# A Perceiver block on one core: the last 65 keys of the first attention as two products of 128 and 97 rows in place of three of 65

## The reference

```python
q = (query @ Wq + bq).reshape(B, L, NKV, G, HDIM)        # 8, 64, 8, 4, 128
k_, v_ = jnp.split(kv @ Wkv + bkv, 2, axis=-1)
scores = jnp.einsum('blkgd,bmkd->bkglm', q, k) * scale
attn = jax.nn.softmax(scores, axis=-1)
o = jnp.einsum('bkglm,bmkd->blkgd', attn, v).reshape(B, L, NHEAD * HDIM)
return o @ Wo + bo
```

## Time and profile before

| | us |
|---|---|
| median of 3 runs (2602.84 to 2605.58) | 2604.69 |
| profiled execution, device time | 2604.12 |
| its span, first to last instruction | 2602.3 |

### The profile page before, as it was taken

How to read it: one execution, slowest core, us unless ns; L and a number is a source line. 1 busy time by engine, 2 the same in 40 slices (tenths; PEclk the granted TensorE clock), 3 DMA queues, 4 the chain that set the end, 5 groups by cost and what they waited for, 6 DMA issues and landing times. The chain is left out here.

```text
span 2602.3 us, 42744 instructions
## 1 busy us (share of the span) xinstructions
PE 2497.1 (96%) x17160; PEld 2293.5 (88%) x17160; DVE 1726.8 (66%) x1956; ACT 1489.4 (57%) x2597; POOL 1348.7 (52%) x1009
## 2 busy tenths in 40 slices
PE   8999999999999999999999999999999599899878
PEld 6899999999999999999999999999987477654557
DVE  4157766777667776677766777667656699743473
ACT  3356655666556665566655666556543677523572
POOL 3335575485565558548556555854600599300352
PEclk9999999999999999999999999999999699999899
DMA  6520011111111101111111110100351300287200
GB/s 221 191 76 31 28 57 52 43 52 54 32 51 51 45 28 58 52 44 51 52 34 51 53 42 26 60 26 29 104 182 54 130 1 1 67 302 266 71 2 17
DMA packets 106989, 181.30 MB, mean 70 GB/s; under 512 B 8852, under 2 KB 72660, under 8 KB 105004
## 3 DMA queue, kind: packets, MB, share of 16 engines
q1 hardware_dynamic: 98476, 170.23, 19.7%
q10 hardware_dynamic: 8320, 8.39, 0.9%
HBM read 158.57 MB, written 20.02 MB: 69 GB/s over the span
## 5 line engine op out<-in xcount | busy, mean ns | idle before, releaser
L474 POOL TENSOR_TENSOR xa_pt_lo<-xs_st,xa_pt_hi 128x1024 fp32r<-128x1024 f32 x255 | 508.4, 2029 | 489.7 <-ACT xa_pt_hi L691 489.7
L54 PE MATMUL ctx_kv_ps<-ctx_wv_hi,ctx_hi 128*128 128x256 f32 x1536 | 431.8, 281 | 0.0
L56 PE MATMUL ctx_kv_ps<-ctx_wv_hi,ctx_lo 128*128 128x256 f32 x1536 | 430.2, 280 | 0.0
L55 PE MATMUL ctx_kv_ps<-ctx_wv_lo,ctx_hi 128*128 128x256 f32 x1536 | 430.2, 280 | 0.0
L54 PE MATMUL ctx_kv_ps<-ctx_hi,ctx_wk_hi 128*128 128x402 f32 (+1 forms) x1024 | 357.7, 349 | 2.4 <-DVE xa_k_lo L791 2.4
L55 PE MATMUL ctx_kv_ps<-ctx_lo,ctx_wk_hi 128*128 128x402 f32 (+1 forms) x1024 | 353.6, 345 | 0.0
L56 PE MATMUL ctx_kv_ps<-ctx_hi,ctx_wk_lo 128*128 128x402 f32 (+1 forms) x1024 | 352.5, 344 | 0.0
L798 DVE TENSOR_TENSOR xa_v_lo<-ctx_kv_ps,xa_v_hi 128x512 fp32r<-128x512 f32 x192 | 132.8, 692 | 244.0 <-ACT xa_v_hi L665 243.4
L55 PEld LDWEIGHTS ctx_kv_ps<-ctx_wv_lo,ctx_hi 128*128 128x128 f32 x1536 | 289.7, 189 | 0.0
L54 PEld LDWEIGHTS ctx_kv_ps<-ctx_wv_hi,ctx_hi 128*128 128x128 f32 x1536 | 288.6, 188 | 0.0
L56 PEld LDWEIGHTS ctx_kv_ps<-ctx_wv_hi,ctx_lo 128*128 128x128 f32 x1536 | 288.4, 188 | 0.0
(11 more groups left out here) (517 smaller groups left out, 6349.3 us busy)
## 6 DMA issues: line engine op xcount, KB each, us to landing
ctx_raw<-in_ctx_t SPq DMA_DIRECT2D x24, 804.0 KB, 6.5
ctx_wk_raw<-in_xa_wk SPq DMA_DIRECT2D x64, 256.0 KB, 2.8
ctx_wv_raw<-in_xa_wv SPq DMA_DIRECT2D x32, 512.0 KB, 4.3
n_back<-in_ctx SPq DMA_DIRECT2D x8, 1280.0 KB, 9.7
q_raw<-in_xa_wq SPq DMA_DIRECT2D x8, 1024.0 KB, 5.0
q_scratch<-q_q_sb ACTq DMA_DIRECT2D x8, 1024.0 KB, 4.5
ctx_q_raw<-q_scratch SPq DMA_DIRECT2D x64, 128.0 KB, 2.7
o_scratch<-xa_o_sb SPq DMA_DIRECT2D x64, 128.0 KB, 1.7
```

The source lines that it names most:

```text
L54: nc.tensor.matmul(out, left[0], right[0], start=first, stop=False)
L55: nc.tensor.matmul(out, left[0], right[1], start=False, stop=False)
L56: return nc.tensor.matmul(out, left[1], right[0], start=False, stop=last)
L474: nc.gpsimd.tensor_tensor(by_chunk(pt_lo, p), scored(j, p).rearrange("p g q c -> p g c q"), by_chunk(pt_hi, p).bitcast(F32), ALU.subtract) ...
```

## The change

The last 65 keys' products are packed. `v_rest` and `pt_rest` have two slots of 128 rows:

- slot 0: rows 0 to 63 `v hi` with `pt hi`, rows 64 to 127 the same `v hi` with `pt lo`, for the first 64 of the 65 keys;
- slot 1: rows 0 to 63 `v lo` with `pt hi`; and for the 65th key row 64 `v hi` with `pt hi`, row 65 `v lo` with `pt hi`, row 96 `v hi` with `pt lo`. Rows between are zero.

So `attend` makes two matmuls over 128 and 97 rows in place of three over 65. For this:

- the pad column of the context is a copy of the last key in place of zero (two more GpSimd instructions of 4 elements a partition at each last tile), so that score row 65 repeats row 64 and the last chunk has 66 rows;
- `keep` rounds and subtracts in the queries' stage, `v_scratch` holds hi and lo, and each `store` is two DMAs;
- `rest_values` on SyncE is six DMAs that put the rows in their places, and on GpSimd one rounding over 128 x 512;
- ScalarE's `high` of the last piece writes both slots, 66 x 512;
- GpSimd's `low` of the last piece is two instructions, from rows 0 to 63 to rows 64 to 127 and from row 64 to row 96, with waits of GpSimd on its own earlier ones;
- the sums leave the last group out of the reduction, and `with_rest` adds its 65 rows in an instruction of its own.

The diff, cut to its core:

```diff
@@ -89,15 +89,24 @@
 
-        for part in (self.hi, self.lo):
-            self.nc.gpsimd.memset(part[:, :, self.S:self.SE].bitcast(F32), 0.0).then_inc(self.pad_set, 1)
-        pool.wait_ge(self.pad_set, 2)
         for t in range(len(self.TILES)):
             pool.wait_ge(self.loaded[t], 16)
-            src, hi, lo = self.parts(t)
-            self.nc.gpsimd.tensor_scalar(hi, src, 1.0, 1.0, ALU.mult, ALU.mult).then_inc(self.hi_set, 1)
-            pool.wait_ge(self.hi_set, t + 1)
-            self.nc.gpsimd.tensor_tensor(lo, src, hi.bitcast(F32), ALU.subtract).then_inc(self.lo_set, 1)
+            self.split(pool, t, t + 1)
+
+    def split(self, pool, t, count):
+
+        nc = self.nc
+        src, hi, lo = self.parts(t)
+        last = t == len(self.TILES) - 1
+        if last:
+            pad = slice(self.S, self.SE)
+            end = src[:, :, self.S - self.TILES[t][0] - 1:self.S - self.TILES[t][0]]
+            nc.gpsimd.tensor_scalar(self.hi[:, :, pad], end, 1.0, 1.0, ALU.mult, ALU.mult)
+        nc.gpsimd.tensor_scalar(hi, src, 1.0, 1.0, ALU.mult, ALU.mult).then_inc(self.hi_set, 1)
+        pool.wait_ge(self.hi_set, count)
+        if last:
+            nc.gpsimd.tensor_tensor(self.lo[:, :, pad], end, self.hi[:, :, pad].bitcast(F32), ALU.subtract)
+        nc.gpsimd.tensor_tensor(lo, src, hi.bitcast(F32), ALU.subtract).then_inc(self.lo_set, 1)
@@ -269,8 +278,13 @@
 
+    LAST = NC - 1
+    REST, ROWS = S - LAST * P, SE - LAST * P
+    EVEN = REST - 1
+    ALONE = 3 * P // 4
+
     def rows(c):
-        return min(P, S - c * P)
+        return min(P, SE - c * P)
@@ -307,8 +321,9 @@
         k_hi, k_lo = sc.sb("k_hi", [P, SE], F32R), sc.sb("k_lo", [P, SE], F32R)
-        v_hi, v_lo = sc.sb("v_hi", [P, NC, 2 * D], F32R), sc.sb("v_lo", [P, NC, 2 * D], F32R)
-        pt_hi, pt_lo = sc.sb("pt_hi", [P, NC, NQ], F32R), sc.sb("pt_lo", [P, NC, NQ], F32R)
+        v_hi, v_lo = sc.sb("v_hi", [P, LAST, 2 * D], F32R), sc.sb("v_lo", [P, LAST, 2 * D], F32R)
+        pt_hi, pt_lo = sc.sb("pt_hi", [P, LAST, NQ], F32R), sc.sb("pt_lo", [P, LAST, NQ], F32R)
+        v_rest, pt_rest = sc.sb("v_rest", [P, 2, 2 * D], F32R), sc.sb("pt_rest", [P, 2, NQ], F32R)
...
@@ -381,11 +398,18 @@
                 n = unit(b, j) // 2
-                r = rows(NC - 1)
-                at = (b + j // NKV) * r
+                at = (b + j // NKV) * REST
+                high, low = (rest.dram[j % NKV // 2, half, at:at + REST] for half in range(2))
                 if n > 0:
                     sp.wait_ge(rest_split, n)
-                sp.dma_start(rest_v[0:r, :], rest.dram[j % NKV // 2, at:at + r]).then_inc(rest_in, 16)
+                else:
+                    sp.wait_ge(rest_clear, 1)
+                sp.dma_start(rest_v[0:EVEN, 0, :], high[0:EVEN]).then_inc(rest_in, 16)
+                sp.dma_start(rest_v[EVEN:2 * EVEN, 0, :], high[0:EVEN]).then_inc(rest_in, 16)
+                sp.dma_start(rest_v[0:EVEN, 1, :], low[0:EVEN]).then_inc(rest_in, 16)
+                sp.dma_start(rest_v[EVEN:REST, 1, :], high[EVEN:REST]).then_inc(rest_in, 16)
+                sp.dma_start(rest_v[REST:ROWS, 1, :], low[EVEN:REST]).then_inc(rest_in, 16)
+                sp.dma_start(rest_v[ALONE:ALONE + 1, 1, :], high[EVEN:REST]).then_inc(rest_in, 16)
@@ -463,24 +487,28 @@
                     apart(pool, passed)
-                    raw, hi, lo = context.parts(t)
-                    nc.gpsimd.tensor_scalar(hi, raw, 1.0, 1.0, ALU.mult, ALU.mult).then_inc(ctx_hi_set, 1)
-                    pool.wait_ge(ctx_hi_set, n * NT + t + 1)
-                    nc.gpsimd.tensor_tensor(lo, raw, hi.bitcast(F32), ALU.subtract).then_inc(ctx_lo_set, 1)
+                    context.split(pool, t, n * NT + t + 1)
 
             def low(b, j, start=0):
-                for p in range(start, NP):
+                for p in range(start, NP - 1):
                     pool.wait_ge(hi_set, unit(b, j) * NP + p + 1)
...
                                             by_chunk(pt_hi, p).bitcast(F32), ALU.subtract).then_inc(lo_set, 1)
+                pool.wait_ge(hi_set, unit(b, j) * NP + NP)
+                pool.wait_ge(lo_set, unit(b, j) * NP + NP - 1 - start)
+                nc.gpsimd.tensor_tensor(pt_rest[EVEN:2 * EVEN, 0, :], rest_scores(j, 0, EVEN),
+                                        pt_rest[0:EVEN, 0, :].bitcast(F32), ALU.subtract).then_inc(rest_low, 1)
+                pool.wait_ge(rest_low, unit(b, j) + 1)
+                nc.gpsimd.tensor_tensor(pt_rest[ALONE:ALONE + 1, 1, :], rest_scores(j, EVEN, REST),
+                                        pt_rest[EVEN:REST, 1, :].bitcast(F32), ALU.subtract).then_inc(lo_set, 1)
+                pool.wait_ge(lo_set, unit(b, j) * NP + NP - start)
 
...
                 n = unit(b, j)
-                r = rows(NC - 1)
-                pool.wait_ge(rest_in, (n // 2 + 1) * 16)
+                pool.wait_ge(rest_in, (n // 2 + 1) * 96)
                 pool.wait_ge(o_full, n + 1)
-                split_on_pool(nc, pool, v_hi[0:r, NC - 1, :], v_lo[0:r, NC - 1, :], rest_v[0:r, :], rest_hi_set,
-                              n // 2 + 1).then_inc(rest_split, 1)
+                nc.gpsimd.tensor_scalar(v_rest[:, :, :], rest_v[:, :, :], 1.0, 1.0, ALU.mult,
+                                        ALU.mult).then_inc(rest_split, 1)
@@ -488,13 +516,16 @@
             def first():
+                nc.gpsimd.memset(rest_v[EVEN:P, 1, :], 0.0).then_inc(rest_clear, 1)
+                pool.wait_ge(rest_clear, 1)
+                nc.gpsimd.memset(pt_rest[EVEN:P, 1, :].bitcast(F32), 0.0).then_inc(rest_clear, 1)
+                pool.wait_ge(rest_clear, 2)
                 for i in range(2):
...
                     pool.wait_ge(early.q_out[i], (NKV // 2 + 1) * 16)
-                nc.gpsimd.memset(ones_r[:, :].bitcast(F32), 1.0)
-                nc.gpsimd.memset(st[:, :, NG - 1, :, :], 0.0).then_inc(ready, 1)
+                nc.gpsimd.memset(ones_r[:, :].bitcast(F32), 1.0).then_inc(ready, 1)
@@ -597,10 +628,13 @@
                         pe.wait_ge(lo_set, unit(b, j) * NP + p)
-                    for c in range(2 * a, min(2 * z, NC)):
-                        r = rows(c)
-                        end = product(nc, o_ps[:, j % 2, 0:NQ], (v_hi[0:r, c, d], v_lo[0:r, c, d]),
-                                      (pt_hi[0:r, c], pt_lo[0:r, c]), c == 0, c == NC - 1)
+                    for c in range(2 * a, min(2 * z, LAST)):
+                        product(nc, o_ps[:, j % 2, 0:NQ], (v_hi[:, c, d], v_lo[:, c, d]), (pt_hi[:, c], pt_lo[:, c]),
+                                c == 0, False)
+                    if p == NP - 1:
+                        nc.tensor.matmul(o_ps[:, j % 2, 0:NQ], v_rest[:, 0, d], pt_rest[:, 0], start=False, stop=False)
+                        end = nc.tensor.matmul(o_ps[:, j % 2, 0:NQ], v_rest[0:ALONE + 1, 1, d], pt_rest[0:ALONE + 1, 1],
+                                               start=False, stop=True)
@@ -688,6 +722,11 @@
                 act.wait_ge(o_full, unit(b, j) + 1)
+                if p == NP - 1:
+                    nc.scalar.activation(pt_rest[0:ROWS, :, :],
+                                         rest_scores(j, 0, ROWS).unsqueeze(1).broadcast_to([ROWS, 2, NQ]),
+                                         ACT.Copy).then_inc(hi_set, 1)
+                    return
@@ -832,10 +871,16 @@
 
+            def with_rest(b, j):
+                dve.wait_ge(sum_main, unit(b, j) + 1)
+                nc.vector.tensor_tensor(sums[0:REST, 1, :], sums[0:REST, 1, :], rest_scores(j, 0, REST),
+                                        ALU.add).then_inc(sum_set, 1)
+
             def summed(b, j):
...
                 dve.wait_ge(sum_lo_set, unit(b, j))
-                over_chunks(sums[:, 1, :], j, 0, NG, ALU.add).then_inc(sum_set, 1)
+                over_chunks(sums[:, 1, :], j, 0, NG - 1, ALU.add).then_inc(sum_main, 1)
+                with_rest(b, j)
@@ -845,11 +890,12 @@
                 else:
-                    over_chunks(sums[:, 0, :], j, PIECES[2][0], PIECES[3][1], ALU.add).then_inc(sum_part, 1)
+                    over_chunks(sums[:, 0, :], j, PIECES[2][0], PIECES[2][1], ALU.add).then_inc(sum_part, 1)
                     dve.wait_ge(sum_part, done + 2)
...
                         dve.wait_ge(sum_lo_set, n)
-                    nc.vector.tensor_tensor(sums[:, 1, :], sums[:, 0, :], m_ps[:, 1, :], ALU.add).then_inc(sum_set, 1)
+                    nc.vector.tensor_tensor(sums[:, 1, :], sums[:, 0, :], m_ps[:, 1, :], ALU.add).then_inc(sum_main, 1)
+                    with_rest(b, j)
...
@@ -1091,12 +1137,13 @@
         sp.wait_ge(self.kept, n + 1)
-        sp.dma_start(self.dram[pairs, self.rows(n)].rearrange("a r n -> r a n"),
-                     self.v_sb[0:r, n % 2].rearrange("r (a n) -> r a n", a=2)).then_inc(self.out[n % 2], 16)
+        for half in range(2):
+            sp.dma_start(self.dram[pairs, half, self.rows(n)].rearrange("a r n -> r a n"),
```

(38 more changed lines are left out.)

## The result

The changed kernel takes **2609.0 us** (median of 14 runs, 2607.35 to 2611.34), the kernel before beside it 2604.46 (14 runs, 2602.81 to 2605.62): a ratio of 1.0018, 95% interval [1.0010, 1.0026], so 4.5 us slower. I had forecast 2600.2, 4.5 us faster. The profiled execution has a span of 2607.0 for 2602.3.

A forecast was written before the change was run, and what follows sets the result against it. TensorE bounds the kernel, busy 96% of the span, so time is its number of matmuls. -7.7 + 1.3 + 0.7 + 1.2 = -4.5 from 2604.12 gives 2599.6, plus 0.6 for the median: 2600.2 us, range 2597.8 to 2603.3.

The forecast's parts named there:

- Matmuls: Attention: one matmul less in each of 64 units at 0.12 us, 7.7 us off; fuller rows cost nothing.
- (a): Queries' stage, `keep(2)`: added subtraction 0.7 us and the second half-store's landing 0.6 delay TensorE's product at 28.24, 1.3 us.
- (b): Queries' stage, `keep(9)`: subtraction ahead of the last `n_xt_lo` costs TensorE 0.7 us (0 to 1.4); n=6 to 8 hidden.
- Behind 43.7 I find no wait of TensorE in this stage: Queries' stage after the first query product at 43.70: no later TensorE wait, so 2.0 us stay lost.
- The port in unit (0,0): Attention's even units: VectorE's two-SBUF-input addition waits 0.2 us for GpSimd's running piece, costing TensorE nothing.
- rival 3: Even units: VectorE's addition lets all GpSimd's pieces go first; TensorE waits 0.4 us in 32 units, 2613 us; chance 0.07.
- the cover of 1.2 us: Even unit: `value_tile(2)` ends at 926.5, TensorE needs its bank at about 927.7, so the addition's delay costs nothing.
- Last unit: Attention's end, TensorE's wait for `sum_lo`: GpSimd's extra 1.0 us plus 0.2 for VectorE's addition, 1.2 us (0.75 to 2.5).
- Between batches: Context split at batch boundaries: GpSimd's additions take 1.3 of the tightest 2.0 us cover, so hidden with 0.7 left.
- the marks that I named: Signs of a wrong prediction: attention, first to last product, shrinks under 6 us, or queries' stage grows over 4.

The follow-up runs named there:

- experiment 1: Kernel before with one of the last chunk's three products left out (64 in all), nothing else changed: 2596.18 us for 2603.85, ratio 0.9971.
- experiment 5: Kernel after with SyncE's 1 MB load of query weights issued behind the ninth pair of stores, not the sixth: 2604.81 us, ratio 1.0004 to the kernel before.
- Experiments 9 and 10: Kernel before with two, then four, idle VectorE copies ahead of the norm's last low part, lengthening TensorE's wait: 2607.97 and 2609.45 us, beside 2603.63.
- experiment 7: Changed attention, before's queries' stage (plain rows stored once), last 65 keys' scores added to the partial sum in PSUM: 2597.45 us, ratio 0.9973 to the kernel before.

## Why the prediction was wrong

- **Matmuls, 7.7 us**: right. 7.7 in experiment 1; in the traces the stretch from the attention's first output product to the wait in the last unit is 8.2 us shorter after and 8.0 in experiment 1, about 0.13 us for each of its 63 products.
- **(a), 1.3 us**: right in kind and nearly in size. The product at 28.24 came at 29.37. But I priced the wait alone; it had grown from 1.22 to 3.32, and the products behind it ran at the low clock, another 1.6 us by 33 us.
- **(b), 0.7 us (0 to 1.4)**: this is the step that failed. TensorE's wait before the first query product grew from 1.67 to 4.20 us, so the term was 2.5. I wrote that `keep` for n=6 to 8 is hidden because VectorE has three instructions of 0.7 us against 2.9 us of products. That counted instructions and not what `keep` waits for: it can't reuse its buffer before the store two `keep`s back has landed. I had priced the doubled store for store 0 alone, and overlooked the 1 MB load that SyncE issues between stores. `keep(8)` waited 3.67 us, and moving the load alone took back 4.2 us of the whole (experiment 5).
- **VectorE's backlog**, also in (b): it fell behind by more than the subtractions. They push its last `xn` beside a GpSimd piece, and there it takes 2.75 us (29.18), 2.75 to 2.78 in all four traces with the subtraction and 1.14 to 1.17 in the eight without. These 1.6 us are in no term of the sum; they are part of why `keep(5)` came 4.3 us later, and the load behind its store 5.2.
- **"Behind 43.7 I find no wait of TensorE in this stage, so 2.0 us stay lost"**: the delay grew from 5.2 to 6.9 and 8.4 us behind waits, by the clock. The sum had no term for it. Experiments 9 and 10 support that term, on average 2.9 us for the one wait lengthened.
- **The port in unit (0,0), priced at nothing**: rival 3's mechanism with another price. The add stood for 2.40 us, and TensorE waited 1.4 us, once. In the usual even unit it took 0.73 us and TensorE didn't wait, so rival 3 itself, in 32 units, did not come. I had taken the cover of 1.2 us from a usual unit; in unit (0,0) there is less, and I hadn't looked.
- **Last unit, 1.2 us**: right as a wait (2.50 for 1.39), and in this trace 1.4 more by the clock.
- **Between batches, hidden**: right; no wait for `ctx_lo`.
- Of the marks that I named, the queries' stage grew by more than 4 (5.2), and the attention from its first to its last output product shrank by 5.8, under my 6, since the last unit's loss is in it.

Summed again in the profiled execution, from the table: +5.2 to the first query product, +1.6 and +1.6 by the clock behind it and at the key tiles, +1.6 in unit (0,0), then -8.2, +2.5 in the last unit and +0.3 behind the attention, which I did not trace: 4.6, against 4.7 at the last product. My 4.5 us of gain were the same sum with 1.3 + 0.7 for the 8.4 of the queries' stage and key tiles, and 1.2 for the 4.1 of unit (0,0) and the last unit.

What stays open is when the clock falls behind a wait. In these twelve traces it fell behind none of the waits up to 1.70 us that are compared here, and behind those of 1.89 to 5.04 us in 20 of 27 cases; the same 2.4 and 2.5 us waits do it in some profiles and not in others. That the low clock explains each kernel's median is shown for none: experiments 9 and 10 show by their medians that a longer wait costs more than its length, and that the excess is the clock's is read from single profiles.

## What to carry to other kernels

Work moved out of a loop into the stage before it is free only if that stage has slack: follow what each moved instruction waits for, buffers and stores included, and what else its DMA queue carries between. Where a stage has one bounding engine, price a longer wait of it as the wait plus what the clock may take behind it. And split a change: here the products left out were worth 7.7 us, and with plain rows, one add's operand in PSUM and one reorder the kernel gains 9.6 (6.0 to 13.0 by its interval): all of the 7.7 by its median, and whether the rest is real isn't shown.

## What the hardware showed that I had not expected

- One row costs GpSimd what 64 do: 741 and 744 ns for 256 columns.
- VectorE's 128x512 `xn`, with one input tile in SBUF and its output there, took 2.75 us when it started at 29.18 beside GpSimd's low pieces (28.05 and 29.28), 1.15 in the kernel before, and 0.55 when alone. So one input in SBUF does not by itself keep a VectorE instruction from being held up, as experiment 7's add alone might suggest.
- The same wait of 2.5 us in the last unit was followed by products at little more than half the pace (0.21 us apart for 0.12) in the kernel after, and by products at full pace in experiment 5. The 1.4 us wait there was never followed by slow ones, in the seven traces that have it.
